# Local attention networks: down products in three reduced passes, one place later, on a kernel of six fused layers

## The reference, cut to what matters

```python
def ffn_layer(x, g, bln, W1, b1, W2, b2):
    mu = x.mean(-1, keepdims=True)
    var = ((x - mu) ** 2).mean(-1, keepdims=True)
    xn = (x - mu) / jnp.sqrt(var + 1e-05) * g + bln
    hg = xn @ W1 + b1
    a, gate = jnp.split(hg, 2, -1)
    return a * jax.nn.gelu(gate, approximate=False) @ W2 + b2
...
x = x + attn_layer(x, ...)
x = x + ffn_layer(x, ...)
```

## Time and profile before

| | us |
|---|---|
| median of 3 runs | 3827.04 |
| lowest and highest run | 3826.9, 3832.35 |
| the profiled execution | 3834.31 |
| its span in the trace | 3832.5 |
| PE busy | 3644.9 (95%) |
| DVE busy | 3115.9 (81%) |
| ACT busy | 2881.7 (75%) |
| POOL busy | 2569.9 (67%) |

### The profile page before, as it was taken

How to read it: one execution, slowest core, us unless ns; L and a number is a source line. 1 busy time by engine, 2 the same in 40 slices (tenths; PEclk the granted TensorE clock), 3 DMA queues, 4 the chain that set the end, 5 groups by cost and what they waited for, 6 DMA issues and landing times. The chain is left out here.

```text
span 3832.5 us, 188979 instructions
## 1 busy us (share of the span) xinstructions
PE 3644.9 (95%) x70894; PEld 2928.2 (76%) x70894; DVE 3115.9 (81%) x8639; ACT 2881.7 (75%) x8501; POOL 2569.9 (67%) x3324
## 2 busy tenths in 40 slices
PE   7869999999999999999999999999999999899998
PEld 4558888688887788876888868888678887566665
DVE  7878888778887788877888868888788887677776
ACT  5758888578886688875888848888578886577776
POOL 3657878478875678755888747887478784455553
PEclk9979999999999999999999999999999999899999
DMA  4023333233333233332333323333233332100000
GB/s 81 1 66 81 80 82 82 60 80 81 81 81 79 61 83 81 81 91 53 80 81 80 81 59 83 82 80 82 69 76 81 81 82 59 34 1 0 0 1 23
DMA packets 307242, 249.24 MB, mean 65 GB/s; under 512 B 74518, under 2 KB 301797, under 8 KB 306277
## 3 DMA queue, kind: packets, MB, share of 16 engines
q1 hardware_dynamic: 307044, 246.78, 26.3%
HBM read 24.47 MB, written 5.24 MB: 8 GB/s over the span
## 5 line engine op out<-in xcount | busy, mean ns | idle before, releaser
L1250 POOL TENSOR_TENSOR wa_t<-wa_t 128x256 f32<-128x256 f32 x1536 | 1093.9, 734 | 343.1 <-DVE wa_t L1043 342.7
L901 ACT ACTIVATE wa_pb<-wa_sc,wa_nm 128x64 f32<-128x64 f32 x3072 | 674.5, 331 | 364.7 <-DVE wa_nm L1088 362.6
L1240 POOL TENSOR_TENSOR wa_t<-wa_t,wa_rn 128x512 f32<-128x512 f32 x768 | 786.0, 1045 | 228.1 <-DVE wa_rn L1066 225.3
L1042 DVE TENSOR_TENSOR wa_t<-wa_pj,wa_ctab 128x512 f32<-128x512 f32 x768 | 529.4, 689 | 207.8 <-PE wa_ta L643 136.7
L46 PE MATMUL wa_pj<-lw_wqkv_high,wa_xhigh 128*128 128x512 f32 x1152 | 533.5, 463 | 35.9 <-DVE wa_t L1043 16.8
L884 ACT ACTIVATE wa_sq<-wa_pj 128x512 f32<-128x512 f32 x768 | 487.0, 636 | 67.7 <-PE wa_pj L48 66.4
L1043 DVE TENSOR_TENSOR wa_t<-wa_pj,wa_stab 128x512 f32<-128x512 f32 x768 | 523.4, 681 | 0.0
L48 PE MATMUL wa_pj<-lw_wqkv_high,wa_xlow 128*128 128x512 f32 x1152 | 461.3, 400 | 0.0
L47 PE MATMUL wa_pj<-lw_wqkv_low,wa_xhigh 128*128 128x512 f32 x1152 | 459.1, 399 | 0.0
L1048 DVE TENSOR_REDUCE wa_raw<-wa_sq 128x16 f32<-128x1024 f32 x384 | 449.5, 1171 | 0.0
L702 PE MATMUL wa_ob<-wa_oT,lw_wo 128*128 128x128 f32 x3120 | 416.9, 277 | 1.9 <-DVE wa_on L1100 1.6
(11 more groups left out here) (304 smaller groups left out, 8195.5 us busy)
## 6 DMA issues: line engine op xcount, KB each, us to landing
wa_vv<-wa_vt SPq DMA_DIRECT2D x2304, 65.0 KB
wa_vv<-wa_vt SPq DMA_DIRECT2D x1152, 32.5 KB
lw_wqkv<-L_ffn_Wqkv SPq DMA_DIRECT2D x6, 1536.0 KB, 6.1
lw_xs<-yT SPq DMA_DIRECT2D x96, 64.0 KB, 1.9
lw_fs<-yT SPq DMA_DIRECT2D x48, 128.0 KB
lw_xs<-yT SPq DMA_DIRECT2D x96, 63.8 KB, 1.9
lw_fs<-yT SPq DMA_DIRECT2D x96, 63.8 KB
bias_by_distance<-dist SPq DMA_DIRECT2D x1, 3072.0 KB, 33.9
```

The costliest lines, as they stand in the source:

```text
L901: last = nc.scalar.activation(pb[:, u.par(2), p, e, :], SC[:, e, p * KEYS:(p + 1) * KEYS], ACT.Exp, bias=nm[:, u.par(2), e, p:p + 1])
L1042: nc.vector.tensor_tensor(t1[:, b, j], x, table(ctab), ALU.mult)
L1240: nc.gpsimd.tensor_tensor(here, here, rn[:, u.par(1), j * HG:(j + 1) * HG].unsqueeze(2).broadcast_to((128, HG, HD)), ALU.mult).then_inc(s. ...
L1250: last = nc.gpsimd.tensor_tensor(here, here, t2[:, b, j, :, of], ALU.add)
```

## The change

- W2 gets high and low parts (`w2p`), which GpSimd makes at the end of the layer's attention, in slots 0 and 1 of the last sequence. The load of W2 gets its own semaphore.
- The product of `gated` goes to a ring of two places in `hid`. ScalarE writes its high part (`hidden_high`), GpSimd its low part (`hidden_low`), and `down` becomes three reduced passes on them. Each down product stands one place later in TensorE's order: chunk 0, down(u-1, 1), chunk 1, norm, down(u-1, 2), turn, chunk 2, down(u, 0).
- VectorE's order becomes gated 0, norm(u+1), gated 1, close(u-1), split(u+1), gated 2, turn(u+2). `turn` also adds epsilon there, into `varp`, after waiting for its own `bn_aggr`; GpSimd is left with the power.
- The high part of the next layer's attention weights moves from GpSimd to ScalarE (`weights_high`).
- To make room in SBUF, the first input's room is freed after phase m0_, and the multiquery weights get tensors of their own in phase n2_; so their seven loads are issued there, ahead of the bias and network loads. `pick` and `band` live only in `modulation`.

```diff
+    w2p=[sb("w2_" + n, [128, GCH, D], F32R) for n in parts]
...
 # TensorE
                 def down(u, j):
                     r = glu_rows(j)
-                    pe.wait_ge(s.act_done, u.n(GCH, j + 1))
+                    pe.wait_ge(s.low_done, u.n(GCH, j + 1))
                     if j == 0 and u.at > 0:
                         pe.wait_ge(s.y_out, u.n(1, 1))
-                    last = nc.tensor.matmul(Y[:, :], w2[0:r, j, :], hid[0:r, j, :],
-                                            start=(j == 0), stop=(j == GCH - 1))
-                    if j == GCH - 1:
-                        last.then_inc(s.down_done, 1)
+                    three_passes(nc, Y[:, :], [x[0:r, j, :] for x in w2p], [high[j][0:r, :], low[(u.par + j) % 2][0:r, :]],
+                                 start=(j == 0), stop=(j == GCH - 1)).then_inc(s.down_done, 1)
                 def multiply(u, turn_later, norm_next, split_next):
                     pe.wait_ge(s.xn_parts, u.n(1, 1))
                     chunk(u, 0)
-                    down(u.before(), 2)
+                    down(u.before(), 1)
                     chunk(u, 1)
                     norm_next()
-                    down(u, 0)
+                    down(u.before(), 2)
                     turn_later()
                     chunk(u, 2)
-                    down(u, 1)
+                    down(u, 0)
...
 # ScalarE
+                def hidden_high(u, j):
+                    act.wait_ge(s.act_done, u.n(GCH, j + 1))
+                    if u.has(1):
+                        act.wait_ge(s.down_done, u.n(GCH, j + 1, 1))
+                    nc.scalar.activation(high[j][0:r, :], hid[0:r, (u.par + j) % 2, :], ACT.Copy).then_inc(s.high_done, 1)
                 def multiply(u, turn_later, norm_next, split_next):
                     gelu(u, 0)
+                    if 1 <= u.at <= NGRP - 2 and not u.final:
+                        weights_high(u)
+                    hidden_high(u, 0)
                     gelu(u, 1)
                     norm_next()
                     split_next()
+                    hidden_high(u, 1)
                     gelu(u, 2)
+                    hidden_high(u, 2)
                 def closing(u, one, two):
                     gelu(u, 0)
                     squares(one, 0)
                     squares(one, 1)
+                    hidden_high(u, 0)
                     gelu(u, 1)
+                    hidden_high(u, 1)
                     values(one)
                     gelu(u, 2)
+                    hidden_high(u, 2)
...
 # VectorE
+                    dve.wait_ge(s.aggr, u.n(1, 1))
+                    nc.vector.tensor_scalar(varp[:, :], mv[:, :, 1], EPS, None, ALU.add).then_inc(s.varp, 1)
...
                 def multiply(u, turn_later, norm_next, split_next):
+                    gated(u, 0)
                     norm_next()
+                    gated(u, 1)
                     close(u.before())
-                    gated(u, 0)
-                    gated(u, 1)
-                    turn_later()
                     split_next()
                     gated(u, 2)
+                    turn_later()
...
 # GpSimd
                 def turn(u):
-                    pool.wait_ge(s.aggr, u.n(1, 1))
+                    pool.wait_ge(s.varp, u.n(1, 1))
...
-                    nc.gpsimd.tensor_tensor(rstd[:, :], mv[:, :, 1], g.eps[:, 0:TPG], ALU.add).then_inc(s.varp, 1)
-                    pool.wait_ge(s.varp, u.n(1, 1))
-                    nc.gpsimd.tensor_tensor(rstd[:, :], rstd[:, :], g.mhalf[:, 0:TPG], ALU.pow).then_inc(s.rstd, 1)
+                    nc.gpsimd.tensor_tensor(rstd[:, :], varp[:, :], g.mhalf[:, 0:TPG], ALU.pow).then_inc(s.rstd, 1)
+                def hidden_low(u, j):
+                    pool.wait_ge(s.high_done, u.n(GCH, j + 1))
+                    if j == 2 or u.at > 0:
+                        pool.wait_ge(s.down_done, u.n(GCH, j - 1))
+                    nc.gpsimd.tensor_tensor(low[(u.par + j) % 2][0:r, :], hid[0:r, (u.par + j) % 2, :], high[j][0:r, :].bitcast(F32),
+                                            ALU.subtract).then_inc(s.low_done, 1)
                 def multiply(u, turn_later, norm_next, split_next):
-                    turn_later()
+                    hidden_low(u.before(), 2)
+                    hidden_low(u, 0)
                     if 1 <= u.at <= NGRP - 2 and not u.final:
                         split_weights(u)
+                    hidden_low(u, 1)
+                    turn_later()
                 def closing(u, one, two):
+                    hidden_low(u.before(), 2)
                     split_input(0, one.sequence(32, 0, 32), one.sequence(4, 0, 1))
+                    hidden_low(u, 0)
                     slot(one)
+                    hidden_low(u, 1)
+                    hidden_low(u, 2)
                     slot(two)
...
 # phase n2_
                 def load(sp, n):
                     if n == 0:
+                        mw.load_weights(sp)
                         mw.load_bias(sp)
                     network.load(sp, n)
```

More of the change, by code:

```diff
@@ L549, in local_layers @@
         gl = gb("gl", [128, 2, GRP])
-        hid = gb("hid", [128, GCH, GRP])
+        hid = gb("hid", [128, 2, GRP])
+        high, low = ([gb(f"hid_{n}{j}", [128, GRP], F32R) for j in range(places)] for n, places in (("high", GCH), ("low", 2)))
         PJ = [ps("pj0"), ps("pj1")]
@@ L858, in whole @@
                     slot(Slot(layer, 4, NB))
-                    down(first, 0)
                     turn(LayerGroup(layer, 2))
                     chunk(first, 2)
-                    down(first, 1)
+                    pe.wait_ge(s.w2_low, 2 * layer + 2)
+                    down(first, 0)
                     groups(pe, layer, multiply, closing, turn, norm)
                     if final:
+                        down(LayerGroup(layer, NGRP - 1), 1)
                         down(LayerGroup(layer, NGRP - 1), 2)
@@ L997, in whole @@
                     norm(LayerGroup(layer, 1))
+                    split(LayerGroup(layer, 1))
+                    hidden_high(first, 0)
+                    hidden_high(first, 1)
                     gelu(first, 2)
-                    split(LayerGroup(layer, 1))
+                    hidden_high(first, 2)
                     groups(act, layer, multiply, closing, None, norm, split)
@@ L1176, in closing @@
                     gated(u, 1)
+                    close(u.before())
                     sums(one)
@@ L1268, in slot @@
                                                 ALU.add).then_inc(s.w1_high, 1)
+                    if u.lead == NB - 1 and u.k < 2:
+                        rows, part = (GW, slice(0, GCH - 1)) if u.k == 0 else (glu_rows(GCH - 1), slice(GCH - 1, GCH))
+                        pool.wait_ge(s.w2_loaded, u.layer * 32 + 32)
+                        nc.gpsimd.tensor_tensor(w2p[0][0:rows, part, :], w2[0:rows, part, :], g.zero[0:rows].unsqueeze(2).broadcast_to(
+                            (rows, part.stop - part.start, D)), ALU.add).then_inc(s.w2_high, 1)
+                        pool.wait_ge(s.w2_high, 2 * u.layer + u.k + 1)
+                        nc.gpsimd.tensor_tensor(w2p[1][0:rows, part, :], w2[0:rows, part, :], w2p[0][0:rows, part, :].bitcast(F32),
+                                                ALU.subtract).then_inc(s.w2_low, 1)
                     if u.lead == 1 and u.k == 3:
@@ L2087, with __init__ @@
 class MultiqueryWeights:
-    def __init__(self, nc, ctx, g, w, room):
+    def __init__(self, nc, ctx, g, w):
         sb = lambda n, s, d=F32: ctx.enter_context(nc.sbuf_tensor("mq_" + n, s, d))
         self.nc, self.g, self.w = nc, g, w
-        flat = room.rearrange("p a t f -> p (a t f)")
-        self.wq, self.wout = flat[:, 0:INNER], flat[:, INNER:2 * INNER].rearrange("p (j n) -> p j n", j=HEADS // 2)
+        parts = ("high", "low")
+        self.wq = sb("wq", [128, INNER])
+        self.wout = sb("wout", [128, HEADS // 2, D])
+        self.wqp = [sb("wq_" + n, [128, INNER], F32R) for n in parts]
+        self.hp = [sb("h_" + n, [128, TOK], F32R) for n in parts]
+        self.bias = sb("bias", [128, HEADS, SEQ])
         self.wkk = sb("wkk", [128, 2, HD])
@@ L2101, in __init__ @@
         self.made += [*self.spread, g.stored]
-    def prepare(self, ctx):
-        sb = lambda n, s, d=F32: ctx.enter_context(self.nc.sbuf_tensor("mq_" + n, s, d))
-        parts = ("high", "low")
-        self.wqp = [sb("wq_" + n, [128, INNER], F32R) for n in parts]
-        self.hp = [sb("h_" + n, [128, TOK], F32R) for n in parts]
-        self.bias = sb("bias", [128, HEADS, SEQ])
     def load_bias(self, sp):
```

78 lines of the change are left out of this document (45 added, 33 removed).

## The result

The changed kernel took **3869.8 us** (median of 4 runs, 3868.2 to 3872.8) against 3828.5 us for the kernel before (median of 4, 3826.9 to 3832.4): a ratio of **1.0107, 95% interval 1.0090 to 1.0125**. It is slower by 41 us, where 27 were forecast: the time lies 16 us above the forecast 3854, inside the range. Of the profiled executions the spans are 3871.1 and 3832.5 us, 38.6 apart.

What follows compares the result with a forecast made beforehand. It took TensorE to bound the kernel before, at 7.76 us a group. Layers 19, last layer 1.9, W2 split 1 and multiquery weights 5.5 sum to 27 us, on the median 3827.04 giving 3854; range 3828 to 3878.

Steps and rivals of the forecast that it cites:

- Part 1: Network stage: three down products save TensorE 0.4 to 0.65 us a group; 7.1 to 7.3 us if it stayed the bound.
- Part 2: Steady groups: a chain of waits from gated 2 to the next group's gated 2 sums to 8.20 us, 8.15 taken.
- the place of the statistics: VectorE's order: statistics behind split and gated 2 delay the power and next norm, making the 8.15 us chain.
- Epsilon: Link from aggregates' end to power: 0.28 us taken for VectorE's new instruction, bounds nothing and 0.72.
- Part 3: Whole layer, engines' instructions laid end to end in both orders: +3.8 us a layer, five times +19.
- First group: First group of a layer's network stage: claimed to change by -0.2 us.
- Closing: End of a layer's stage: +3.4 us, with GpSimd late three times, by about 1.55, 0.6 and 0.6.
- The last layer: No closing there; a high part, a low part and a product in line behind group 7's gelu 2: +1.9 us.
- Part 5: Multiquery weights loaded in phase n2_, GpSimd waiting for them: +5.5 us; sign, the phase longer by 3 to 8.
- rival B: VectorE's split waits for GpSimd: at a whole 1.25 us, 0.65 a group more, 3877 us; chance 0.14.
- A: TensorE stays the bound, faster: 3811 us, chance 0.09, or 3828 with a costly closing, chance 0.09.
- C: The 8.15 us chain holds, but GpSimd's lateness is taken back before the next layer: 3836 us; chance 0.10.

Runs made afterwards that it cites:

- e8_order_four: The changed kernel with the same work in a new order on all four engines inside a group: 3859.7 us, ratio 1.0072.
- e3_order_alone: The kernel before, with only VectorE's statistics moved behind split and gated 2, without the high and low parts: 3876.9 us, ratio 1.0123.
- e1_turn_first: The changed kernel with VectorE's statistics put back in front of split and gated 2: 3888.6 us, ratio 1.0160.
- e2_norm_first: The changed kernel with VectorE's norm in front of gated 0 and statistics in front of split and gated 2: 3872.5 us, ratio 1.0109.
- e6_two_ends: The changed kernel with GpSimd's closing order changed and Wq's load on its own semaphore: 3855.6 us, ratio 1.0072.

## Why the prediction was right, and where it was not

The mechanism came as forecast, a ring over four engines and two later ends, and the time lies inside the range. Part of the nearness is luck: the layers lost 15.6 us more than forecast, and errors in other terms hid 4.4 of them.

- **Part 1, TensorE's work:** right. 36.96 us busy for five groups against 38.81, and 7.3 us a group in e8_order_four, where the ring is open.
- **Part 2, the ring:** right in kind and nearly in size. The sum of rows was 8.20, 8.15 was taken; the turns measure 8.42 and 8.23 in alternation. Their terms, with the prediction's in brackets: gated 2 to statistics 0.67 (0.66), statistics to the aggregates' end 1.30 (1.30), to the power 0.28 or 0.40 (0.28), power and handoff 1.26 or 1.05 (1.05), norm to scale and shift 2.34 or 2.22 (2.27), from there to gated 2 2.57 or 2.60 (2.64). The larger excess lies in norm: in the turn of 8.42 it stands behind gated 0 of group 3, which starts 0.67 us after VectorE was free (721.80 above, though gelu 0 had ended at 721.10) and is the first instruction of a new turn of the engine's loop; in the other, norm waits for the power, as forecast. Gaps of 0.43, 0.19 and 0.25 us stand before gated 0 of groups 2, 4 and 5 too. The trace names no cause for them, and none was tried: it stays open.
- **"What made the difference is the place of the statistics":** enough to close a ring in the kernel before (e3_order_alone), but wrong as what holds this one (e1_turn_first). Putting them back costs 0.4 to 0.8 us a group, putting norm in front as well leaves it at 8.36 (e2_norm_first). The ring depends on the order of all four engines together: one other order of the same instructions takes 7.3 us.
- **Epsilon:** its 0.28 was right for this order in half the turns. It is a price of the place, not of the instruction: 0.17 us with GpSimd idle, up to 0.74 beside it. The upper bound of 0.72 was a price of the place too: with GpSimd's epsilon in this order the way takes 0.36 to 0.48, since no low part of VectorE stands beside it.
- **Part 3, a layer:** +3.8 forecast, +6.8 measured. Head -1.1 (-1.1 measured). First group -0.2: +0.1 with the clock full and +1.0 to +1.3 where it fell; the prediction left the clock open in its last sentence and put no price on it. What it asked there, whether the clock stays full with a microsecond of idle time a group, is answered yes for groups 2 to 6 (1.00, also in e3_order_alone); it fell at the head. Four groups of +0.34: +0.5 each; the last of the five, without statistics, +0.3: +0.9, 7.78 for 6.87. The statistics behind gated 2 of group 5 still hold the norm in group 6, and TensorE waits 0.84 us for it at 748.69, so the ring runs through this group too. The clock and the five groups are the largest mis-sized terms. Closing +3.4: +3.4, with waits of 1.40, 0.41 and 0.60 for the 1.55, 0.6 and 0.6 forecast.
- **The last layer,** +1.9: +3.3. The clock fell in its group 1 (+1.1 there) and its groups lost more, as above; its end lost 0.9.
- **Part 5,** +5.5: +2.7. The loads landed 6.7 us after the first issue, not 9, since seven issues took 3.34 us here, for 7.5 in the earlier trace rows. The phase grew by 2.7, just under the 3 to 8 that the prediction named as its sign. e6_two_ends shows that the wait for all seven was the whole loss: with Wq alone 3.1 us come back.
- **The rule of the skill** (rival B) was given 0.14 on the ground that 842 ns was the most that any low part took the earlier trace rows. The instructions do exclude each other; the order keeps the ones that are held up from meeting on the ring. A chance for it was right, the reason against it was a misreading: the low parts of 822 to 842 ns met a GpSimd instruction with under 0.3 us left and ended 0.55 us after it, as the held ones of e8_order_four do, so these were whole holds of a short remainder. A stronger row was left unread: GpSimd's epsilon of 0.42 to 0.56 us beside VectorE's low part, for 0.20 alone, in the same trace.
- **Rivals A and C** are out: TensorE waits 4 us in five groups, and the closing's loss stays, since the five layer periods grew by 34.2 us in sum.

Together: 15.6 us too little on the layers, 5 of them the clock's, 2.8 too much on the loads and 1.6 gained elsewhere are the 11.2 us between the sum's 27.4 and the measured 38.6.

## What to carry to other kernels

When the bound engine's work is cut, lay out the ring from one step of the loop to the next before counting the saving: here 0.45 us a group was on offer and 0.5 was lost, and an order laid out anew on all four engines, priced with durations from the trace, gave 7.3 us where moving VectorE's steps alone gave nothing. Then look at the two ends of the stage, which here weighed as much as the steady part, and look for SBUF work of VectorE that comes to stand beside a GpSimd instruction: its price is what is left of that instruction.

## What the hardware showed that was not expected

- VectorE and GpSimd hold each other up until the other's instruction ends, in both forms tried: a sum of 4 columns takes 0.16 to 0.17 us with GpSimd idle and up to 0.74 beside it, a sum of 64 columns 0.21 and 1.31, a low part of 512 columns 0.69 and up to 1.58 (e3_order_alone). Such a low part ends 0.54 to 0.56 us after the GpSimd instruction that it meets, in all 123 instances of these traces in which that one had 0.27 us or more left; GpSimd's power is the exception, with 66 of 66 low parts not held up by its last 0.32 to 0.56 us. An instruction of VectorE with one input in PSUM (gated, with 0.74 to 0.75 us) shows none of it, whether GpSimd is busy or not.
- GpSimd pays in the same way. Its epsilon, 0.20 us alone, ends 0.06 us after the low part of VectorE that it meets, and its power, 1.01 us alone, 0.87 us after it, in every one of the 30 instances each (kernel before, e2_norm_first). Both differences are 0.14 us: by this estimate about that much of a GpSimd instruction passes while it is still held up.
- TensorE's clock fell to 1.2 GHz for some 3.4 us behind waits of 1.15 and 0.58 us in 18 of 36 stages, and never in the six when they were filled; it stayed at 1.00 in groups where TensorE waited 4.06 of 41.02 us or 5.9 of 46.01. Whether it falls changes from layer to layer of one execution, with the same waits in front.
